# Grouped attention on TensorE: scores in two halves around a transposed block, and the weighted values of two units in two places

## The reference

```python
def _L0_attn_ref(x, wq, wk, wv, wo):
    ...
    q = (x @ wq).reshape(b, s, NH, HD)
    k = (x @ wk).reshape(b, s, NKV, HD)
    v = (x @ wv).reshape(b, s, NKV, HD)
    k = jnp.repeat(k, NREP, axis=2)
    v = jnp.repeat(v, NREP, axis=2)
    scores = jnp.einsum('bihd,bjhd->bhij', q, k) * SCALE
    causal = jnp.tril(jnp.ones((s, s), dtype=bool))
    scores = jnp.where(causal, scores, jnp.finfo(scores.dtype).min)
    attn = jax.nn.softmax(scores, axis=-1)
    out = jnp.einsum('bhij,bjhd->bihd', attn, v)
    ...
x = L0_attn_x
...
h = _layernorm(x, axis=-1) * (1 + ca) + sa
x = x + ga * _L0_attn_ref(h, L0_attn_wq, L0_attn_wk, L0_attn_wv, L0_attn_wo)
h = _layernorm(x, axis=-1) * (1 + cb) + sb
x = x + gb * _L0_ffn_ref(h, L0_ffn_A_w, L0_ffn_B_w, L0_ffn_Wq_w, L0_ffn_keys)
```

## Time and profile before

| | |
|---|---|
| median of 3 runs | 902.42 us (901.54 to 904.47) |
| profiled execution, its own time | 901.53 us |
| its span | 899.7 us |
| PE, DVE, ACT, POOL busy over the span | 854.0, 679.4, 533.0, 193.8 us |
| scores of unit 0 start | 79.3 us |
| weighted values of unit 63 end | 257.4 us |

### The profile page before, as it was taken

One profiled execution on the slowest core, in us unless ns is written; L12 is line 12 of the kernel. 1 busy time (PEld: TensorE's weight loads), 2 busy tenths in 40 slices (PEclk: granted clock), 3 DMA queues, 4 the chain that ended last, 5 costly groups with the idle time before them and its releaser, 6 DMA issues.

```text
span 899.7 us, 13681 instructions
## 1 busy us (share of the span) xinstructions
PE 854.0 (95%) x5096; PEld 674.5 (75%) x5096; DVE 679.4 (76%) x1067; ACT 533.0 (59%) x717; POOL 193.8 (22%) x199
## 2 busy tenths in 40 slices
PE   3998999999989998999999999999989999999997
PEld 1566777777767786788888887888867888888886
DVE  4736888889998788598888885777885876667852
ACT  4412777777664542866666665677464876666840
POOL 3003567668855034000000000000310000000004
PEclk9898999999999999999999999999999999999999
DMA  9678579887841032025333333233221442332202
GB/s 321 222 223 164 63 101 137 138 127 96 156 144 49 30 96 71 34 83 151 106 106 105 106 94 94 67 98 94 70 71 48 137 119 90 101 94 71 70 1 94
DMA packets 38450, 95.35 MB, mean 106 GB/s; under 512 B 7144, under 2 KB 10216, under 8 KB 37360
## 3 DMA queue, kind: packets, MB, share of 16 engines
q1 hardware_dynamic: 35840, 90.68, 41.2%
q10 hardware_dynamic: 2544, 3.79, 1.2%
HBM read 79.56 MB, written 2.21 MB: 91 GB/s over the span
## 4 chain that ended last, share of the span: by engine, by line
PE 54%; DVE 10%; ACT 5%; issue 2%; POOL 2%; POOLq 0%; DVEq 0%; ACTq 0%
PE PS L1690 11%; PE PS L1691 11%; PE PS L1692 11%; PE PS L2007 5%; PE PS L2006 5%; PE PS L2008 5%; DVE ACC L1280 2%; POOL X L803 2%; DVE ST L1200 1%; ACT PL L929 1%; DVE SCR L1265 1%; ACT XM L898 1%; PE PS L1991 1%; PE PS L1979 1%; ACT FH L898 1%
## 5 line engine op out<-in xcount | busy, mean ns | idle before, releaser
L929 ACT ACTIVATE PL<-CODE 128x1024 f32<-128x1024 int32 x200 | 202.2, 1055 | 60.6 <-DVE ACC L1280 58.0
L1690 PE MATMUL PS<-HH,WRH 128*128 128x512 f32 x448 | 175.8, 392 | 6.2 <-DVE HL L1235 3.1
L1691 PE MATMUL PS<-HH,WRL 128*128 128x512 f32 x448 | 175.2, 391 | 0.0
L1692 PE MATMUL PS<-HL,WRH 128*128 128x512 f32 x448 | 174.9, 390 | 0.0
L803 POOL TENSOR_TENSOR X<-X,SCR 128x512 f32<-128x512 f32 x32 | 43.9, 1378 | 545.1 <-DVE SCR L1265 544.6
L1280 DVE SCALAR_TENSOR_TENSOR ACC<-PL,ACC 128x1024 f32<-128x1024 f32 x100 | 123.6, 1236 | 9.3 <-DVE ACC L1280 1.4
L977 ACT ACTIVATE PT<-PS 128x512 f32<-128x512 f32 x160 | 86.3, 604 | 43.2 <-PE PS L1812 22.1
L820 POOL TENSOR_TENSOR QS<-ident,MX 64x256 fp32r<-64x256 f32 x128 | 97.9, 765 | 54.4 <-DVE MX L1445 34.7
L1690 PEld LDWEIGHTS PS<-HH,WRH 128*128 128x128 f32 x448 | 84.5, 189 | 25.9 <-DVE WRL L1292 3.4
L1692 PEld LDWEIGHTS PS<-HL,WRH 128*128 128x128 f32 x448 | 84.5, 189 | 17.8
L1691 PEld LDWEIGHTS PS<-HH,WRL 128*128 128x128 f32 x448 | 84.5, 189 | 16.8
(11 more groups left out here) (232 smaller groups left out, 1529.0 us busy)
## 6 DMA issues: line engine op xcount, KB each, us to landing
CODE<-in_CODES SPq DMA_DIRECT2D x50, 512.0 KB, 3.5
SCALE<-in_SCALES SPq DMA_DIRECT2D x100, 256.0 KB, 4.0
WM<-in_WM SPq DMA_DIRECT2D x12, 1024.0 KB, 6.7
QS<-FQ SPq DMA_DIRECT2D x32, 256.0 KB, 6.5
KS<-KHL SPq DMA_DIRECT2D x32, 64.0 KB, 5.3
KN<-KHL SPq DMA_DIRECT2D x32, 64.0 KB, 4.5
GAB<-gates SPq DMA_DIRECT2D x4, 512.0 KB, 3.8
out_x<-X ACTq DMA_DIRECT2D x8, 256.0 KB, 2.0
```

What stands on the lines that cost most here:

```text
L929: nc.scalar.activation(PL[:, n % 3], CODE[:, p % 2], ACT.Prelu, scale=scale, bias=bias, alpha=alpha).then_inc(s_plane, 1)
L1690: nc.tensor.matmul(dst, lh, rh, start=start and k == 0, stop=False)
L1691: nc.tensor.matmul(dst, ll, rh, start=False, stop=False)
L1692: ins = nc.tensor.matmul(dst, lh, rl, start=False, stop=stop and k == KC - 1)
```

## The change

Three things change in the order on TensorE, and nothing else in the program.

- `scores(n, half)` gives one half, and the turn calls it twice.
- The transposed blocks of unit `n - 3` are laid out in three places: ahead of the first half, between the halves, and behind the second. For units of 1, 2, 3, 4 key blocks these are 0 + 0 + 1, 0 + 1 + 1, 1 + 1 + 1 and 2 + 1 + 1 blocks.
- In odd turns the weighted values of unit `n - 5` stand between the halves, behind that transposed block, and those of unit `n - 4` at the turn's end as before.

```diff
-            def scores(n):
+            def scores(n, half):
                 q, ic = divmod(n, TB)
-                if ic == 0:
+                if ic == 0 and half == 0:
                     pe.wait_ge(s_qks[q % STACKS], 96 * (q // STACKS + 1))
-                for half in range(2):
-                    if n >= 1:
-                        pe.wait_ge(s_mx, 2 * (n - 1) + half + 1)
-                    for h in (2 * half, 2 * half + 1):
...
+                if n >= 1:
+                    pe.wait_ge(s_mx, 2 * (n - 1) + half + 1)
+                for h in (2 * half, 2 * half + 1):
...
             for n in range(units + TURN + 1):
-                early = EARLY if (n - TURN) % TB == TB - 1 else 0
+                ic = (n - TURN) % TB
+                first, second = ((0, 0), (0, 1), (1, 2), (2, 3))[ic]
                 if TURN <= n < units + TURN:
-                    transposed(n - TURN, 0, early)
+                    transposed(n - TURN, 0, first)
                 if n < units:
-                    scores(n)
+                    scores(n, 0)
                 if TURN <= n < units + TURN:
-                    transposed(n - TURN, early, TB)
-                if n >= TURN + 2 and n % 2 == 1:
-                    for unit in (n - TURN - 2, n - TURN - 1):
-                        weighted(unit)
+                    transposed(n - TURN, first, second)
+                turn = n >= TURN + 2 and n % 2 == 1
+                if turn:
+                    weighted(n - TURN - 2)
+                if n < units:
+                    scores(n, 1)
+                if TURN <= n < units + TURN:
+                    transposed(n - TURN, second, TB)
+                if turn:
+                    weighted(n - TURN - 1)
```

More of the change, by code:

```diff
@@ L1786, in _ @@
             blocks = [0, 0]
-            def scores(n):
+            def scores(n, half):
                 q, ic = divmod(n, TB)
-                if ic == 0:
+                if ic == 0 and half == 0:
                     pe.wait_ge(s_qks[q % STACKS], 96 * (q // STACKS + 1))
-                for half in range(2):
-                    if n >= 1:
-                        pe.wait_ge(s_mx, 2 * (n - 1) + half + 1)
-                    for h in (2 * half, 2 * half + 1):
[L1796 to L1801, removed]
+                if n >= 1:
+                    pe.wait_ge(s_mx, 2 * (n - 1) + half + 1)
+                for h in (2 * half, 2 * half + 1):
+                    ins = nc.tensor.matmul(PS[:, h, 0:(ic + 1) * P], QS[:, q % STACKS, h, ic * P:(ic + 1) * P],
+                                     KS[:, q % STACKS, 0:(ic + 1) * P], start=True, stop=True)
+                    if ic not in ADDED_MASK:
+                        ins = nc.tensor.matmul(PS[:, h, ic * P:(ic + 1) * P], identR, maskR[:], start=False, stop=True,
+                                               skip_group_check=True)
+                ins.then_inc(s_s, 1)
             def transposed(n, first, last):
```

## The result

The changed kernel takes 907.4 us (median of 4 runs, 906.87 to 907.77) against 902.19 us before (4 runs, 901.54 to 904.47); the ratio is 1.0054, 95% interval [1.0039, 1.0069]. By the ratio it is slower by 4.9 us, where 3.0 were forecast. The mechanism for the seven turns of the odd sums came out within 0.02 us a turn; the price of a burst of weighted values and a wait on ScalarE did not. (A burst is a run of weighted values that stand one behind the other.)

The account below looks back on a forecast made before the run. TensorE and VectorE were taken to set the attention loop's pace in turn. Terms -1.0 + 2.0 + 2.2 + 0.1 - 0.3 = +3.0 us on 901.53, plus 0.9 to the median: 905.4 us, range 898.5 to 909.5.

Parts of the forecast that it names:

- The sums of the odd group: Units 13, 21 to 61: first value burst waits for VectorE's sums; 3.50 against 3.21 us, seven times, +2.0 us.
- The gain of 0.13 in the other eight pieces: Units 5, 9, 17 to 57: a transposed block fills TensorE's stop before scores; 3.08 against 3.21 us, -1.0 us.
- The second half behind the values: Unit 7 of eight: second half of scores comes 0.67 us later, VectorE stands 0.37; six times, +2.2 us.
- Unit 3 of eight hidden: Same late second half at unit 3 of eight, covered by VectorE's division or gate of 0.7 us; no cost.
- Exponentials: Transposed blocks spread out: TensorE's 2.9 us of waits for exponentials shrink a little; -0.3 us, ends 0 and -2.9.
- The added switches: 31 more value bursts on TensorE: 0.13 each plus 0.10 to switch, in the walked pieces' sums; elsewhere covered or 0.
- no difference: Rival: the late second half is absorbed, as VectorE has other reasons to be late; 903.1 us, chance 0.26.
- faster: Rival: the new order fills TensorE's stops and no new wait binds; 897.5 us, chance 0.24.
- Slower by more: Rival: TensorE is the pace in nearly every piece and the added switches are not covered; 908.9 us, chance 0.12.

Follow-up runs that it names:

- bursts alone: Against the kernel before: only the first unit's weighted values moved ahead of the turn's last transposed block, 31 bursts more; 908.82 us, ratio 1.0064.
- two blocks ahead: Changed kernel with both units' values at the turn's end and, at unit 5 of eight, two transposed blocks ahead of the scores, one between; 897.13 us, ratio 0.9938.

## Why the prediction was right or wrong

- *The sums of the odd group, forecast +2.0 us:* right. Pieces of 3.48 to 3.52 us against 3.50 forecast, the burst 0.06 behind the sums, seven times; together 1.95 us over before. The run with the sums first takes the wait away, and the run without that turn's values brings the change back to no difference.
- *The gain of 0.13 in the other eight pieces, forecast -1.0 us:* wrong, and the largest miss, 2.0 us; they came out at +1.0 in sum. At unit 5 the piece is 3.07 (forecast 3.08). At units 17, 25, 33, 49 and 57 it is 3.17 to 3.31, at 9 and 41 it is 3.71 and 3.72. The step that failed is the one that took all eight pieces to be "without a new wait", since the even side "has no such place". For the bank that is true. But ScalarE copies the even group out of it just ahead of these turns, and the exponentials stand behind the copy in its queue. The transposed block that now stands ahead of the first burst needs one of them. Unit 9 in the changed kernel, ScalarE and then TensorE:

```profile
99.07 0.60 ACT L977 ACTIVATE PT<-PS 128x512 f32<-128x512 f32 x1 [2.28 <-PE PS L1814]
99.56 1.05 ACT L929 ACTIVATE PL<-CODE 128x1024 f32<-128x1024 int32 x1
100.51 0.68 ACT L624 ACTIVATE NUM<-PS,HALVES 128x512 f32<-128x512 f32 x1
101.08 0.69 ACT L624 ACTIVATE DEN<-PS,HALVES 128x512 f32<-128x512 f32 x1
101.65 2.07 ACT L977 ACTIVATE PT<-PS 128x512 f32<-128x512 f32 x4
```

```profile
101.42 0.50 PE L1795 MATMUL PS<-KS,QS 128*128 128x256 f32 x2
102.31 0.49 PE L1811 MATMUL PS<-QS,KN 128*128 128x512 f32 x1 [0.39 <-ACT PT L977]
```

  Before, that block stood behind four heads and another block, and the delay was covered. The prediction looked for who waits for the bank, and forgot who waits behind the one that empties it. About 0.2 us a piece goes with the copy (unit 17's 3.27 against unit 5's 3.07, where no copy is due). The other 0.43 at units 9 and 41 comes from the turn of unit 7 of eight: the single transposed block there now stands behind three value blocks, so ScalarE stands 2.28 us for it at 99.07, has a curve and the copy still to do, and starts the exponentials 0.23 behind unit 9's scores. With turn 7's values at the end it stands 1.53 us and starts them 0.19 ahead, and the piece is 3.28. This second cost of the values at unit 7 of eight the prediction did not have.
- *The second half behind the values, forecast +2.2 us at unit 7 of eight:* the mark was right at four of the six places (VectorE idle 0.40 or 0.41 us at units 15, 23, 39 and 55, forecast 0.37; 0.16 at unit 7 and 0.03 at unit 47), and unit 31, whose piece was forecast 0.1 longer, has 0.41 as well and a piece 0.34 longer. The sum is near (the pieces from 6 to 9 grew by 1.8 us, forecast 2.3 with unit 31), the cause only half right. With the values behind both halves the idle is gone and the piece is longer still (7.36 against 7.24). TensorE's own stream with one burst more is about as long as VectorE's delayed one, so either would have set nearly the same time. How much of the 1.8 us is each one's cannot be told from these runs.
- *Unit 3 of eight hidden, forecast 0:* wrong by 1.0 us. The idle was 0 at units 3, 27, 43 and 51, 0.04 at 11, but 0.41, 0.34 and 0.19 at 19, 35 and 59, and the pieces from unit 18 and unit 50, which TensorE paces, grew by 0.14 and 0.15. I had given TensorE a microsecond of slack in every such piece, read from one of them.
- *Exponentials, forecast -0.3 us:* did not come. From 79 to 258 us TensorE's matmuls idle 3.6 us for them after, and 3.4 us before.
- *The added switches:* mis-sized, 0.23 us forecast for a burst, 0.30 to 0.35 measured. To the 0.13 of a burst and the 0.10 to enter it comes 0.1 for what stands behind it. In the forecast's own pieces the error did no harm, by luck: its 0.35 for the second half was read behind another half, and behind values a half costs just that (0.34), while between two blocks it costs 0.26. The rule of the Trainium skill in "TensorEngine Tiling (Array Packing)", Key Properties, that a change of tiling mode drains the engine, fits the direction: bursts alone cost 5.8 us. No row shows the drain itself, and the weighted values also differ from their neighbours in number format (`V` and `PT` are F32, `QS`, `KS` and `KN` F32R); no run tells the two apart.
- *The rivals:* "no difference" and "faster" fell. "Slower by more" had a true cause, TensorE as the pace in more pieces than I gave it, and at 908.9 us lay 1.5 us above the result, where the forecast lay 2.0 below. Of "faster" one half was true: the moved block does fill a stop, and without the moved values the same idea is 4.8 us faster than before.
- *The sum:* the pieces of the loop grew by 5.7 us in the profiles, 2.7 more than forecast: about 2.0 from the eight pieces, 1.0 from unit 3 of eight and 0.3 from the exponentials, less 0.5 that unit 7 of eight was overpriced.

## What to carry to other kernels

When a step is moved up in one engine's queue, ask two questions of everything it waits for: when that is done, and what else stands in the queue of the engine that does it. A block that fills a stop is worth its whole length, but a burst of another kind of matmul (here 32-column tiles and F32) costs its entry and its exit each time it is cut off from its like, 0.3 us here; keep such bursts together and fill stops with matmuls of the same kind as their neighbours.

## What the runs showed of the hardware that was not expected

- Two heads of 256 columns take 0.34 us behind weighted values and 0.26 us between two transposed blocks (turn 13, above). In these rows the price of a matmul depends on its neighbours, not on its shape alone.
- At the loop's beginning the granted clock is at its lower level (0.50, 1.2 GHz) for some microseconds in all profiles but one, and where that falls differs from profile to profile; with one profile for each kernel it is open whether the edit or the single execution decides it. Before, the means were 0.62 and 0.70 from 80 to 85 and 85 to 90 us, and 1.00 from 90 on; with two blocks ahead the clock was 1.00 from 80 to 95. With bursts alone TensorE ran at full clock from 85 to 90 us and at a mean of 0.66 from 90 to 95; in the three microseconds before it fell, at 91, the engine was busy for 1.9. So unit 5's piece took 4.96 instead of 3.56 us there, while the piece ahead of it took 7.94 instead of the 8.49 of before. That is 0.85 us net over before for which the bursts do not account.

```profile
85.00:90.00 5.00, 3.82 (x17) 2.50 (x17) 4.97 (x7) 0.97 (x2) 2.83 (x4) 1.00 0.65 67
90.00:95.00 5.00, 4.54 (x34) 2.40 (x33) 3.17 (x17) 2.36 (x6) 3.73 (x6) 0.66 0.00 0
```
